# A causal attention kernel with a gated feed-forward end: the feed-forward part rewritten over all engines and begun in the last pair of heads

## The reference

```python
q, k, v = x @ Wq, x @ Wkv[:, :1024], x @ Wkv[:, 1024:]      # split into 16 heads of 64
s = einsum('bhid,bhjd->bhij', q * 64**-0.5, k)
p = where(causal_mask, 0.0, exp(s - max(s, axis=-1)))        # the maximum is taken over all columns
a = (p @ v) / (sum(p) + 1e-8)
x = layernorm(x + a @ Wo + bo)
# feed-forward part
x_prev = x moved by one token (zeros at the start of each batch)
r = sigmoid((mu_r*x + (1-mu_r)*x_prev) @ W_r.T)
k = (mu_k*x + (1-mu_k)*x_prev) @ W_k.T
out = layernorm(x + r * (square(relu(k)) @ W_v.T))
```

## Time and profile before

| | |
|---|---|
| Time, median of 3 runs | 1128.13 us (1126.86 to 1128.16) |
| The profiled execution's own time | 1127.08 us |
| Its span, first to last instruction | 1125.3 us |
| Mean granted TensorE clock | 0.983 |
| Busy: PE / PEld / DVE | 1042.6 / 675.1 / 931.2 us |
| Busy: ACT / POOL | 740.5 / 564.9 us |
| Last scores of the last pair end on PE | 1027.7 us |
| First feed-forward product (W_k, batch 0) | 1059.9 us |
| Last compute instruction ends (DVE) | 1121.65 us |

### The profile page before, as it was taken

The page is one execution under the profiler, slowest core; times in us unless marked ns, Lnnn a source line. Parts: engine busy times, 40 slices in busy tenths (PEclk is TensorE's granted clock), DMA queues, the critical chain, the costliest instruction groups (busy, mean ns, idle before and its releaser), DMA issues.

```text
span 1125.3 us, 21967 instructions
## 1 busy us (share of the span) xinstructions
PE 1042.6 (93%) x7411; PEld 675.1 (60%) x7411; DVE 931.2 (83%) x1588; ACT 740.5 (66%) x1666; POOL 564.9 (50%) x902
## 2 busy tenths in 40 slices
PE   7899999999999999999999999999999999997653
PEld 5566666666666666666666666666666666654442
DVE  5988888888888888888888888888888888888397
ACT  5777666676677666766677666766666667665354
POOL 5355565555555665555555655555556655542200
PEclk9999999999999999999999999999999999999887
DMA  5355556655455555554455565544555565545311
GB/s 157 80 114 123 132 122 137 141 119 120 110 119 125 128 129 141 131 116 116 111 125 129 123 141 137 119 116 115 119 126 128 132 142 126 120 111 125 84 38 37
DMA packets 74193, 134.05 MB, mean 119 GB/s; under 512 B 26849, under 2 KB 36833, under 8 KB 74081
## 3 DMA queue, kind: packets, MB, share of 16 engines
q1 hardware_dynamic: 73504, 132.26, 50.3%
q10 hardware_dynamic: 576, 0.39, 0.1%
HBM read 21.17 MB, written 2.36 MB: 21 GB/s over the span
## 4 chain that ended last, share of the span: by engine, by line
PE 62%; DVE 19%; issue 11%; ACT 4%; POOL 1%; SPq 1%; DMA 1%; DVEq 0%; ACTq 0%; POOLq 0%
PE ps_s L775 26%; PE ps_x L829 22%; DVE tile L600 7%; DVE stage L609 7%; PE ps_x L788 6%; PE ps_x L840 4%; PE ps_x L711 2%; ACT pt L506 2%; ACT full L467 1%; DVE stats L624 1%; POOL tile L363 1%; SPq L315 1%; ACT tile L459 1%; DVE recips_sb L619 1%; DVE pt L646 1%
## 5 line engine op out<-in xcount | busy, mean ns | idle before, releaser
L600 DVE TENSOR_SCALAR_CACHE_REDUCE tile<-ps_s 128x1024 f32<-128x1024 f32 x512 | 606.7, 1221 | 153.2 <-PE ps_s L775 149.7
L459 ACT ACTIVATE tile<-tile,neg_max 128x640 f32<-128x640 f32 (+7 forms) x512 | 397.2, 777 | 211.8 <-POOL tile L363 211.7
L775 PE MATMUL ps_s<-ks,qs 64*128 64x512 f32 x3072 | 424.7, 408 | 11.0 <-DVE tile L600 7.7
L363 POOL TENSOR_SCALAR_AFFINE_SELECT tile<-tile 128x128 f32<-128x128 f32 x512 | 149.9, 293 | 454.3 <-DVE tile L600 453.4
L775 PEld LDWEIGHTS ps_s<-ks,qs 64*128 64x128 f32 x3072 | 269.4, 184 | 131.0 <-issue 49.4
L829 PE MATMUL ps_x<-pt,vs 128*64 128x256 f32 (+1 forms) x2560 | 270.4, 362 | 0.1
L609 DVE STREAM_TRANSPOSE stage<-tile 128x640 f32<-128x640 f32 (+3 forms) x256 | 253.5, 1019 | 0.1
L829 PEld LDWEIGHTS ps_x<-pt,vs 128*64 128x64 f32 x2560 | 173.6, 137 | 108.4 <-issue 34.9
L788 PE MATMUL ps_x<-ident,tile 128*128 128x128 f32 x640 | 117.8, 290 | 13.6 <-ACT full L467 11.9
L788 PEld LDWEIGHTS ps_x<-ident,tile 128*128 128x128 f32 x640 | 69.3, 140 | 96.8 <-issue 43.5
L711 PE MATMUL ps_x<-xs,ws 128*128 128x512 f32 x381 | 119.2, 422 | 0.3 <-DVE xs L575 0.3
(11 more groups left out here) (75 smaller groups left out, 559.4 us busy)
## 6 DMA issues: line engine op xcount, KB each, us to landing
pt<-stage SPq DMA_DIRECT2D x512, 120.0 KB, 3.3
pt<-stage SPq DMA_DIRECT2D x512, 88.0 KB, 2.1
rb<-recips SPq DMA_DIRECT2D x64, 256.0 KB, 4.1
out<-y SPq DMA_DIRECT2D x4, 512.0 KB, 3.2
y<-in_L_attn_x SPq DMA_DIRECT2D x3, 512.0 KB, 8.2
pt<-in_L_attn_Wkv SPq DMA_DIRECT2D x2, 384.0 KB, 6.4
pt<-in_L_attn_x SPq DMA_DIRECT2D x2, 256.0 KB, 4.3
wos<-in_L_attn_Wo SPq DMA_DIRECT2D x1, 512.0 KB, 7.2
```

The lines of the kernel that those rows point to most:

```text
L363: pool.affine_select(out=block_of, in_=block_of, compare_op=ALU.is_ge, fill=fill, base=0, pattern=[[-1, P]], channel_multiplier=1).then_in ...
L459: act.activation(cols, cols, ACT.Exp, bias=neg_max[:, at:at + 1], scale=-1.0, accum_out=sums[:, p % 2, a, t:t + 1]).then_inc(s_exp, 1)
L600: dve.tensor_scalar(tile[:, at, :], ps_s[scores_at(p, t, a)][:, :], -SCALE, None, ALU.mult, ALU.min, accum_out=neg_max[:, at:at + 1]).then ...
L775: ins = mm(ps_s[scores_at(p, t, a)][:, c * HALF:(c + 1) * HALF], qs[rows, p % 2, qh, t * P:(t + 1) * P], ks[rows, p % 2, kh, c * HALF:(c + ...
```

## The change

It rewrites everything after the last pair, and puts the start of it into the last pair:

- The extra round of the loops goes. In the last pair, steps 0 to 3, at the places of the missing q and k projections, TensorE turns the sums of batches 0 and 1 in four halves into `ps_x` banks (`turn_half`), and ScalarE copies them back over `y` (`take_sums`). VectorE takes the first moments of batch 0 at step 4 of the last pair.
- The first norm is halved: VectorE norms tiles 0 to 3 and ScalarE tiles 4 to 7 (Identity with a scale and a bias for each token; the bias, `shift`, is a new small VectorE instruction). The second norm is ScalarE's alone, but halved in the last batch.
- The result of the first norm lies in `y`. Only one mixed copy is left (`mix_r`): for W_k, `mu_k` and `1 - mu_k` are multiplied into two copies of the weights (`ffn_k`), and TensorE adds two products, with the tokens and with the tokens before (4 products of 512 columns for a batch, before 2).
- relu moves from ScalarE to VectorE; the square and the addition of x move from VectorE to GpSimd (`square`, `add_gated`).
- The rest of the last pair's attention work (its last `values`, `norm`, `project_out`, `add_out`) is put between the instructions of batches 0 and 1.
- Some steps hand on halves of 512 columns where they were whole before. Batches 2 and 3 have their sums turned in the loop, in `ps_s[0]`.

```diff
 def users_of_banks(p, t):
+    if t in QK_AT and p == LAST:
+        users.append(("sum", *divmod(QK_AT[t], 2)))
@@ sync
             for b in range(B):
-                sp.wait_ge(f_fin, b + 1)
+                sp.wait_ge(f_fin[1], b + 1)
+                if b == B - 1:
+                    sp.wait_ge(f_fin[0], 1)
@@ gpsimd
+            norm(LAST - 1, 1)
+            add_out(LAST - 1, 1)
+            norm(LAST, 0)
+            for b in range(B):
+                square(b)
+                if b == 0:
+                    add_out(LAST, 0)
+                if b == 1:
+                    norm(LAST, 1)
+                add_gated(b)
+                if b == 1:
+                    add_out(LAST, 1)
@@ scalar
+            def take_sums(b, c):
+                act.wait_ge(f_sums, 2 * b + c + 1)
+                act.activation(y[:, b * N + c * HALF:b * N + (c + 1) * HALF], ps_x[BANK["sum", b, c]][:, :], ACT.Copy
+                               ).then_inc(f_yt, 1)
+            def first_norm(b):
+                act.wait_ge(f_shift, norms_before(b, 0) + 1)
+                for t in range(4, TILES):
+                    ins = act.activation(normed[b][:, t, :], sums_of(b)[:, t, :], ACT.Identity,
+                                         bias=shift[0][:, t:t + 1], scale=rstd[0][:, t:t + 1])
+                ins.then_inc(f_x1[1], 1)
+            def second_norm(b):
+                act.wait_ge(f_shift, norms_before(b, 1) + 1)
+                for t in range(4 if b == B - 1 else 0, TILES):
+                    ins = act.activation(normed[b][:, t, :], normed[b][:, t, :], ACT.Identity,
+                                         bias=shift[1][:, t:t + 1], scale=rstd[1][:, t:t + 1])
+                ins.then_inc(f_fin[1], 1)
@@ vector
+                    if p == LAST and t == 4:
                         first_moments(0)
+            recips_of(LAST)
+            first_norm(0)
+            turn_tile(LAST, TILES - 1, 0)
+            turn_tile(LAST, TILES - 1, 1)
...
+            for b in range(B):
+                if b + 1 < B:
+                    first_norm(b + 1)
+                for c in range(2):
+                    dve.wait_ge(f_k, 2 * b + c + 1)
+                    dve.tensor_scalar(act_k[:, c * HALF:(c + 1) * HALF], tokens_in[:, c * HALF:(c + 1) * HALF],
+                                      0.0, None, ALU.max).then_inc(f_relu, 1)
+                for c in range(2):
+                    dve.wait_ge(f_sig, 2 * b + c + 1)
+                    dve.wait_ge(f_v, 2 * b + c + 1)
+                    part = gate[b % 2][:, 4 * c:4 * c + 4, :]
+                    dve.tensor_tensor(part, part, tokens(tokens_in[:, :])[:, 4 * c:4 * c + 4, :], ALU.mult
                                       ).then_inc(f_gate, 1)
+                moments(b, 1, normed[b])
+                if b + 1 < B:
+                    mix(b + 1)
+                factors(b, 1)
+                if b + 2 < B:
+                    first_moments(b + 2)
+                if b == B - 1:
+                    normed_half(b, 1, normed[b], f_fin[0])
@@ tensor
+            pe.wait_ge(s_evac, SLOTS * ALL_PAIRS)
+            project_out(LAST - 1, 1)
+            turn_normed(0)
+            project_out(LAST, 0)
+            for b in range(B):
+                project_k(b)
+                if b == 2:
+                    turn_sums(3)
+                project_r(b)
+                if b == 0:
+                    values(LAST, 1, (2,))
+                project_v(b)
                 if b == 1:
+                    project_out(LAST, 1)
+                if b + 1 < B:
+                    turn_normed(b + 1)
+                if b == 0:
+                    turn_sums(2)
+                    values(LAST, 2, (3,))
```

More of the change, by code:

```diff
@@ L158, in build @@
         rstd = [sb(f"rstd{n}", [P, TILES]) for n in range(2)]
+        shift = [sb(f"shift{n}", [P, TILES]) for n in range(2)]
         ps_s = [psum(f"ps_s{n}", [P, N]) for n in range(NSCORES)]
@@ L234, in build @@
         f_rstd = sem("f_rstd")
-        f_x1 = sem("f_x1")
+        f_shift = sem("f_shift")
+        f_x1 = [sem(f"f_x1{c}") for c in range(2)]
         f_x1t = sem("f_x1t")
@@ L247, in build @@
         f_sum = sem("f_sum")
-        f_fin = sem("f_fin")
+        f_fin = [sem(f"f_fin{c}") for c in range(2)]
         f_w = sem("f_w")
@@ L511, in _ @@
                         take_values(p - 2, 2)
[L512 removed]
+                    if t == 6:
                         take_values(p, 0)
@@ L637, in normed, with normed_half @@
+            def normed_half(b, half, src, done):
+                for t in range(4):
+                    ins = dve.tensor_scalar(normed[b][:, t, :], src[:, t, :], mv[half][:, t, 0:1],
+                                            rstd[half][:, t:t + 1], ALU.subtract, ALU.mult)
                 ins.then_inc(done, 1)
             def first_moments(b):
-                dve.wait_ge(f_yt, b + 1)
-                moments(b, 0, tokens(ps_s[0][:, :]))
-            def mixes(b):
-                for n, mix in enumerate((mix_r, mix_k)):
-                    dve.wait_ge(f_prev, 2 * b + n + 1)
-                    dve.scalar_tensor_tensor(out=mix[b % 2], in0=x1t[:, 1:N + 1], scalar=small[:, n:n + 1],
-                                             in1=mix[b % 2], op0=ALU.mult, op1=ALU.add).then_inc(f_mix, 1)
@@ L649, in _, with first_norm, mix @@
-            for p in range(ALL_PAIRS + 1):
+                dve.wait_ge(f_yt, 2 * b + 2 if b < 2 else b + 3)
+                moments(b, 0, sums_of(b))
+            def first_norm(b):
+                factors(b, 0)
+                normed_half(b, 0, sums_of(b), f_x1[0])
+            def mix(b):
+                dve.wait_ge(f_prev, b + 1)
+                dve.scalar_tensor_tensor(out=mix_r, in0=x1t[:, 1:N + 1], scalar=small[:, 0:1], in1=mix_r,
+                                         op0=ALU.mult, op1=ALU.add).then_inc(f_mix, 1)
@@ L858, in _, with turn_half @@
-            for p in range(ALL_PAIRS + 1):
-                for t in range(TILES):
-                    if p < ALL_PAIRS:
-                        scores(p, t)
-                    if t in TURN_FIRST and p < ALL_PAIRS:
+            def turn_half(b, c):
+                drained(("sum", b, c))
+                bank = ps_x[BANK["sum", b, c]]
+                for n in range(2):
+                    pe.wait_ge(s_yadd[n], PAIRS * (b + 1))
+                for t in range(4):
+                    at = b * N + c * HALF + t * P
+                    ins = turn(bank[:, t * P:(t + 1) * P], y[:, at:at + P], ident[:, :])
+                ins.then_inc(f_sums, 1)
@@ L863, in _ @@
+            for p in range(ALL_PAIRS):
+                for t in range(TILES):
+                    scores(p, t)
+                    if t in TURN_FIRST:
                         turn_tile(p, TURN_AT[t], 0)
-                    if t in V_AT and p < ALL_PAIRS:
+                    if t in V_AT:
                         v_of(p // 2, 2 * (p % 2) + V_AT[t])
```

287 lines of the change are left out of this document (144 added, 143 removed).

## The result

| | before | changed |
|---|---|---|
| Time, median of 4 runs on one chip | 1127.77 us (1126.86 to 1128.16) | 1115.05 us (1114.68 to 1116.2) |
| Ratio, with its 95% interval | | 0.9883 (0.9871 to 0.9894) |
| Profiled execution: own time, span | 1127.08, 1125.3 us | 1115.07, 1113.3 us |
| Mean granted TensorE clock | 0.983 | 0.989 |
| Last compute instruction ends | 1121.65 us (VectorE) | 1109.63 us (ScalarE) |

The account below looks back on a forecast made before the run. After the last pair, a hole until 1060, then four 16.3 us batches that VectorE carries nearly alone. Last compute at 1106.5 plus 3.65 gives span 1110.15; own time 1.8 above, median 1.05 above that: 1113.0 us, range 1108 to 1120.

Parts of the forecast that it names:

- The hole and the head start: After the last pair: TensorE still waits for the reciprocals, but W_k of batch 0 starts at 1048.15 instead of 1059.88, 11.7 us.
- +0.6 us for the whole of it: Last pair: added turned sums, copies and batch 0's moments delay it 0.6 us, at least 0.45, at most 2.65.
- The late transposes of tile 7: VectorE, after the last pair: they end about 3 us later, near 1037.6, hidden because SyncE's last moves started only at 1040.17.
- TensorE's stretch: 1046.05 to 1070.2: TensorE's products, turns and attention work follow one another, partly at the lower clock; the other engines keep up.
- ScalarE's norm piece: 128-column norm piece on ScalarE: taken as 0.32 us; 0.15 would give 2.5 us less, 0.41 would give 1.8 more.
- The end: From the second half of batch 2's gate (1090.5) to the last compute (1106.5): 16.0 us.
- GpSimd late: Rival, batches: GpSimd's halves take 1.9 instead of 1.25 us, adding about 5.5 us, so 1118.5 us; chance 0.12.
- Only the head start: Rival: batches stay at 16.3 us, passing work through four engines in turn; only 11.7 us gained, 1116.4 us; chance 0.06.
- TensorE at the lower clock: Rival, from 1048 on: TensorE's 41 us of work become 82, time 1145 us; chance 0.03 slower than before, 0.01 within.
- 3.5 in the prediction: Clock uncertainty after the last pair: if TensorE's clock were never low, the time would be 3.5 us less.
- VectorE's mix beside an addition: Batches: by the skill's rule the mix could lose up to 1.25 us beside GpSimd's addition, 3.8 us in three batches.
- 1.05 above it: Last term of the sum: the median of the runs lies 1.05 us above the profiled execution's own time, 1111.9.

Follow-up runs that it names:

- e2: Changed kernel with all the last pair's attention work put ahead of batch 0 again, the rest of the change kept: 1124.71 us, 0.9968 of the kernel before.
- e1: Changed kernel with all four halves of sums, their copies and batch 0's moments behind the last pair again: 1113.75 us, 0.9875 of the kernel before.
- e8: Changed kernel with only batch 0's sums turned in the last pair, batch 1's two halves behind it: 1114.88 us, 0.9882 of the kernel before.
- e7: Changed kernel with the square back on VectorE and relu back on ScalarE, the addition still on GpSimd: 1117.49 us, 0.9907 of the kernel before.
- e4: Changed kernel plus unread TensorE transposes, 60 in the hole and 34 before W_v of batch 2: 1112.38 us, 0.9861 of the kernel before.
- e10: Changed kernel with batch 0's W_k, W_r before project_out(31, 0), batch 1's sums behind the pair, last sigmoid before batch 2's second norm, 34 unread transposes: 1103.77 us.
- e5: Changed kernel with VectorE's relu of a batch ahead of its half of the next batch's first norm: 1117.65 us, 0.9907 of the kernel before.
- e6: Changed kernel with the last sigmoid ahead of batch 2's second norm, that norm halved between VectorE and ScalarE: 1114.11 us, 0.9877 of the kernel before.

## Why the prediction was right, and where its sum was short

- **The hole and the head start: right.** `project_out(31, 0)` starts at 1046.96 behind 7.39 us idle (forecast 1046.05, 8 us), W_k of batch 0 1.87 us later (2.1). e2 prices the head start at 9.7 us and the batches at 3.6; the prediction had 11.7 and the rest of 15, some 3.4. The start of W_k moved by 11.05, but the 7.1 us of attention work that went in among the batches did not all hide. My later expectation of 5 us for it was further off than the prediction.
- **"+0.6 us for the whole of it" in the last pair: mis-sized.** It is 0.9 in every trace up to the last `values`, and 1.16 to the projection in this one (e1, e8). The moments on VectorE, which I counted, cost nothing; the copy behind ScalarE's exponential, which I counted as mostly hidden, costs 0.7 of it. A further 0.34 us is that pair 31 itself began at 1000.37 and not at 1000.03 in these two executions; in all thirteen profiled ones it began between 999.89 and 1000.48.
- **The late transposes of tile 7, "hidden": right.** They end at 1038.73 (forecast 1037.6), and SyncE's last 16 moves start only at 1041.63, directly behind the queue's earlier issues.
- **TensorE's stretch: right.** Forecast starts of W_k 1048.15, 1064.7, 1075.9 and 1091.7; measured 1048.83, 1065.21, 1077.13 and 1093.20. The steps between them are 16.4, 11.9 and 16.1 against 16.55, 11.2 and 15.8. In batch 1 VectorE's half of the norm waits 1.33 us for a square root that stands behind ScalarE's second norm of batch 0 (until 1068.08); the sum had relu at 1068.9, and it came at 1070.00.
- **ScalarE's norm piece, "I take 0.32": mis-sized.** It is 0.40 in a row and 0.48 alone. The estimate from the Trainium skill, page "ScalarE: Activation LUTs", section "What ACT_TABLE_LOAD costs", was 0.39: the trace agrees with it (0.40, 3.21/8). In the final second norm that is 0.65 us, in the last four pieces 0.36 more (1.66 against 1.3).
- **The end, "16.0": mis-sized.** From the second half of batch 2's gate (1091.90) to the last compute (1109.63) it is 17.7. Beside the 1.0 us of norm pieces, the square root of batch 2 waits for the table load behind the mixed copy (1095.25), 0.3 us; the rest, some 0.4 us, lies in the steps between.
- **GpSimd late: refuted.** Its square takes 1.04 us, less than the 1.25 taken, its addition 1.25. In e7, where the square is VectorE's and the relu ScalarE's, the kernel is slower.
- **Only the head start (1116.4): refuted as it stood**, since the batches gave 3.6 us; but its reason held. VectorE's work fell from 54.73 us in the last 65.3 to 10 or 11 a batch (10.11 between W_k of batches 2 and 3; the forecast was under 10), and the round stayed near 16: ScalarE's second norms start 15.8 and 16.5 us apart, and the periods are 15.6 and 16.9 in e2, where no attention work stands between the batches. The 11.9 us of batch 1 in the changed kernel are no shorter round: TensorE, busy with attention work, had begun its W_k late. The chain of waits of the changed kernel shows the ring that took its place:

```profile
1078.72 1.28 ACT L478
...
1080.79 3.21 ACT y L510 x8
...
1084.70 1.28 DVE y L717 x4
1085.98 0.61 DVE pt L773
...
1086.65 1.05 POOL pt L405
...
1087.74 3.70 PE ps_s L983 x16
```

  Table load, second norm of one batch, first norm of another, relu, square, W_v, gate: each is short, and each waits for the one before. e4 and e10 show that W_v is part of it: 1.5 us less there made the period 1.5 shorter, though TensorE, with the 34 turns, had more to do in all. e5 shortened the same period by 1.3 us by relu's place in the queue. That the pieces of GpSimd and ScalarE count in the same way is read from the chain; no edit tested each of them alone.
- **TensorE at the lower clock: refuted as a case, right as a cost.** Keeping the clock up gave 3.3 us in its rows and 2.4 in the time, against 3.5 in the prediction; the turns that kept it up and a later norm took 1.0 back (e4).
- **VectorE's mix beside an addition.** The rule of the Trainium skill, page "SBUF — State Buffer", section "Who interferes with whom", cost nothing here, since the mix of batch 2 starts at 1078.74, 0.37 us after the addition ends; but it holds (below).

The sum was behind by 0.7 us at W_k of batch 0 (0.56 from the pair's halves and 0.34 from its offset, less 0.2 on the way), by 1.5 at W_k of batch 3 and by 3.1 at the last compute. A tail of 3.67 us behind the last compute and 1.77 of own time above the span came as forecast; the median of the changed kernel lay on its profiled execution, not 1.05 above it, which takes one of the 3.1 back.

## What to carry to other kernels

Taking work off the busiest engine shortens a round only until the ring of hand-overs binds; read the chain of waits of one period and ask which instruction stands ahead of the one that the next engine needs. A small job put into a pipelined stage can cost more by the bank that it holds while its copy queues than by its length (here 0.9 us for two halves, while two others cost nothing). Work whose operands are ready belongs ahead of an instruction that waits for a DMA, not behind it (here 6 us for moving one line).

## What was not expected of the hardware

**VectorE and GpSimd on SBUF.** In four places a VectorE instruction with its operands in SBUF took longer beside a GpSimd one, the long ones by up to nearly their full time, the shift until GpSimd's ended: the half norm in e6 2.12 instead of 1.11 us (above); in e1 the mix 2.15 instead of 1.28 us beside a multiplication that ends at 1045.26, and a half norm 2.06 beside an addition; in e5 the shift of 8 columns 1.00 instead of 0.17 (above), until GpSimd's square ends at 1072.29. The rows of e1, VectorE and GpSimd:

```profile
1038.19 2.06 DVE L717 TENSOR_SCALAR y<-y,mv,rstd 128x128 f32<-128x128 f32 x4
...
1044.19 2.15 DVE L732 SCALAR_TENSOR_TENSOR pt<-x1t,small,pt 128x1024 f32<-128x1024 f32 x1 [1.84 <-ACT pt L497]
```
```profile
1038.39 1.26 POOL L393 TENSOR_TENSOR y<-y,ot 128x512 f32<-128x512 f32 x1 [4.63 <-ACT ot L560]
1043.74 1.52 POOL L386 TENSOR_TENSOR ot<-ot,rb 128x512 f32<-128x512 f32 x1 [4.09 <-DMA rb<-recips]
```

GpSimd's own instructions keep their length here. The Trainium skill, page "SBUF — State Buffer", section "Who interferes with whom", says that two SBUF inputs make VectorE contend with GpSimd's reads; the mix and the shift agree. The same section of the Trainium skill says that a `tensor_scalar` can enter a mode that takes both ports; the half norm from SBUF (2.06 and 2.12 us) agrees with that. Relu, which reads PSUM, lost nothing in the changed kernel: one half alone takes 0.69 us (from 1051.47), and two in a row take 1.28 (from 1097.20), although GpSimd's square runs beside the second from 1097.96 on. In three of the four places GpSimd had started first, and in the fourth, the half norm of e1, only the first of four pieces stood ahead of it; what happens when VectorE starts first no run here separates.

**GpSimd's square.** With both operands the same tile it takes 1.04 us for 512 columns, the addition of two tiles 1.27, the multiplication with a strided operand 1.52 (1.57 in the median of the kernel before).
